# Two of the four heads' products of P by the inverse row sums move from GpSimd to VectorE

## The reference

```
scores = einsum(q, k) * 32 ** -0.5          # the first has 4 heads of k and v, each for 4 of q
scores = where(causal, scores, -inf)
attn   = softmax(scores, axis=-1)
out    = einsum(attn, v)                    # then @ Wo, added to x
```

## Time and profile before

| | |
|---|---|
| median of three runs | 3520.3 us (3517.94 to 3524.21) |
| profiled execution | 3521.41 us, of which the span of the core is 3519.6 us |
| stage a0 (22 to 457 us of the span) | 435 us, PE busy 353.4, DVE 172.3, ACT 258.8, POOL 315.8 |
| stage a1 (883 to 1360 us) | 477 us, PE busy 418.8, DVE 176.0, ACT 276.0, POOL 319.1 |

### The profile page before, as it was taken

One profiled execution on the slowest core, in us unless ns is written; L12 is line 12 of the kernel. 1 busy time (PEld: TensorE's weight loads), 2 busy tenths in 40 slices (PEclk: granted clock), 3 DMA queues, 4 the chain that ended last, 5 costly groups with the idle time before them and its releaser, 6 DMA issues. The chain is left out here.

```text
span 3519.6 us, 46857 instructions
## 1 busy us (share of the span) xinstructions
PE 3027.7 (86%) x16388; PEld 2286.1 (65%) x16388; DVE 1881.8 (53%) x5092; ACT 1556.4 (44%) x3598; POOL 1261.5 (36%) x1399
## 2 busy tenths in 40 slices
PE   6788789997899985887868875998779999989999
PEld 4666567886666663544646754776367777768887
DVE  4434267777443334323466667665577787753221
ACT  4666656665566554123322225443545555541000
POOL 4877823222576673000016761000033333313222
PEclk8889899998999996889989987999889999999999
DMA  2000030102000003021110011000300000020000
GB/s 84 1 1 1 1 119 31 32 31 78 1 1 1 1 1 123 26 72 59 66 57 4 4 42 57 1 1 34 113 1 1 1 1 1 1 99 12 12 13 13
DMA packets 65872, 105.51 MB, mean 30 GB/s; under 512 B 9315, under 2 KB 29795, under 8 KB 65509
## 3 DMA queue, kind: packets, MB, share of 16 engines
q1 hardware_dynamic: 65222, 102.41, 8.4%
q0 software_dynamic: 416, 0.10, 0.0%
HBM read 89.75 MB, written 12.85 MB: 29 GB/s over the span
## 5 line engine op out<-in xcount | busy, mean ns | idle before, releaser
L661 POOL TENSOR_SCALAR a_P<-a_P,a_rec 128x384 f32<-128x384 f32 (+3 forms) x512 | 548.2, 1093 | 241.4 <-DVE a_rec L816 241.4
L402 ACT ACTIVATE tree_value<-tree_bit,table_lut,tree_step 128x256 f32<-128x256 uint8 x496 | 275.7, 595 | 138.0 <-DVE tree_value L416 71.9
L416 DVE COPY_PREDICATED tree_value<-tree_bit,tree_value 128x256 f32<-128x256 uint8 x434 | 234.3, 547 | 133.7 <-ACT tree_value L402 105.3
L893 PE MATMUL bank<-ident,a_P 128*128 128x128 f32 x1280 | 200.4, 307 | 114.8 <-POOL a_P L661 112.5
L810 DVE CUSTOM_DVE_ANT_0 a_P<-bank,a_causal 128x384 f32<-128x384 f32 (+3 forms) x512 | 221.6, 480 | 123.3 <-PE bank L883 123.3
L732 ACT ACTIVATE a_P<-a_P,a_low 128x384 f32<-128x384 f32 (+3 forms) x512 | 281.2, 556 | 13.4 <-DVE a_low L810 13.3
L101 PE MATMUL bank<-f_xT_hi,f_w_hi 128*128 128x512 f32 (+1 forms) x704 | 276.1, 392 | 8.1 <-DVE f_w_lo L1145 8.1
L1069 POOL CAST f_h_hi<-f_sg 128x512 fp32r<-128x512 f32 (+1 forms) x88 | 85.1, 967 | 548.4 <-DVE f_sg L1166 277.6
L102 PE MATMUL bank<-f_xT_hi,f_w_lo 128*128 128x512 f32 (+1 forms) x704 | 275.7, 392 | 0.0
L103 PE MATMUL bank<-f_xT_lo,f_w_hi 128*128 128x512 f32 (+1 forms) x704 | 275.5, 391 | 0.0
L893 PEld LDWEIGHTS bank<-ident,a_P 128*128 128x128 f32 x1280 | 164.5, 158 | 149.1 <-POOL a_P L661 124.6
(11 more groups left out here) (451 smaller groups left out, 7824.3 us busy)
## 6 DMA issues: line engine op xcount, KB each, us to landing
f_w_raw<-in_f_w SPq DMA_DIRECT2D x11, 768.0 KB, 12.5
f_w_raw<-table_w SPq DMA_DIRECT2D x11, 768.0 KB, 11.2
tree_idx<-in_f_idx SPq DMA_DIRECT2D x62, 128.0 KB, 2.1
table_w<-tree_value SPq DMA_DIRECT2D x62, 128.0 KB, 1.7
x_res<-in_x SPq DMA_DIRECT2D x4, 1024.0 KB, 11.0
m_piece<-in_m_wq SPq DMA_DIRECT2D x2, 2048.0 KB, 12.2
m_piece<-in_m_wo SPq DMA_DIRECT2D x2, 2048.0 KB, 8.7
m_piece<-in_m_w_gate SPq DMA_DIRECT2D x2, 2048.0 KB, 10.8
```

The lines of the kernel that those rows point to most:

```text
L402: act.activation(prog.tree_value[(h + to) % 4][:, :], prog.tree_bit[h % 2][0][:, :], ACT.Identity, bias=prog.table_lut[:, 2 * k:2 * k + 1] ...
L416: dve.copy_predicated(prog.tree_value[(h + keep) % 4][:, :], prog.tree_bit[h % 2][bit][:, :], prog.tree_value[(h + other) % 4][:, :]).then ...
L661: last = pool.tensor_scalar(Pr[j][:, g, col:col + n], Pr[j][:, g, col:col + n], rec[:, j, i, g:g + 1], None, ALU.mult)
L893: last = pe.transpose(ps[J.bank(key)][:, g * P:(g + 1) * P], Pr[j][:, g, col + kt * P:col + (kt + 1) * P], prog.ident[:, :])
```

## The change

On POOL the loop over heads at L661 now runs over heads 2 and 3 only. On DVE the entry `rec`, behind the reciprocal, waits for it and multiplies P of heads 0 and 1, in place, with the same instruction that POOL used, and counts a new semaphore `p_scaled_dve`. The first transpose of a chunk waits for both. The entry for DVE's products stands inside `rec`, so `low` of n + 2 for heads 2 and 3 now comes after them.

```diff
@@ gpsimd
                     pool.wait_ge(*c_rec(0, at + 1))
-                    for g in range(G):
+                    for g in range(G // 2, G):
                         for i, (col, qt) in enumerate(PARTS[j]):
                             n = (qt + 1) * P
                             last = pool.tensor_scalar(Pr[j][:, g, col:col + n], Pr[j][:, g, col:col + n], rec[:, j, i, g:g + 1], None, ALU.mult)
@@ vector
                     dve.wait_ge(*c_exp(0, G * (at + 1)))
                     dve.reciprocal(rec[:, j, 0:parts, :], total[:, j, 0:parts, :]).then_inc(c_rec.sem, 1)
+                    dve.wait_ge(*c_rec(0, at + 1))
+                    for g in range(G // 2):
+                        for i, (col, qt) in enumerate(PARTS[j]):
+                            n = (qt + 1) * P
+                            last = dve.tensor_scalar(Pr[j][:, g, col:col + n], Pr[j][:, g, col:col + n], rec[:, j, i, g:g + 1], None, ALU.mult)
+                    last.then_inc(c_own.sem, 1)
@@ tensor
                     if at == FIRST[3 * m + j]:
+                        pe.wait_ge(*c_own(0, 3 * m + j + 1))
                         pe.wait_ge(*c_scaled(0, 3 * m + j + 1))
```

More of the change, by code:

```diff
@@ L593, in attention32 @@
     c_whi, c_wlo, c_xhi, c_xlo = (prog.count(n) for n in ("w_hi", "w_lo", "xT_hi", "xT_lo"))
-    c_qk, c_exp, c_scaled, c_pv = (prog.count(n) for n in ("qk_hi", "p_exp", "p_scaled", "pv"))
+    c_qk, c_exp, c_scaled, c_own, c_pv = (prog.count(n) for n in ("qk_hi", "p_exp", "p_scaled", "p_scaled_dve", "pv"))
     c_ot_hi, c_ot = (prog.count(n) for n in ("ot_hi", "ot_lo"))
@@ L942, in attention32 @@
     c_scaled.advance(CHUNKS)
+    c_own.advance(CHUNKS)
     c_pv.advance((PER - 1) * NU)
```

## The result

The changed kernel took 3396.6 us (median of four runs, 3395.84 to 3405.19), against 3521.9 us before: a ratio of 0.9651, 95% interval 0.9633 to 0.9669. That is 125 us less; the prediction was 3415 us, 106 less, with a range of 3375 to 3480.

What follows compares the result with a forecast made beforehand. PE was taken as the bound, idle in both attentions mostly for POOL's products of P. Waits 96 plus clock 25 less cost 15 gave 106 us saved, 3521.4 - 106 = 3415 us; range 3375 to 3480.

Steps and rivals of the forecast that it cites:

- What bounds it: In both attention stages, a0 and a1, PE's waits for POOL's product of P make 112.5 of 140 us idle.
- The price on DVE: DVE's new products beside POOL: 0.78 us each at 512 columns; 146 us over 32 units, 91 if nothing collides.
- The rule that spoke against it: Shared SBUF ports as exclusive lock: each DVE product in a0 and a1 would wait out a POOL product of 1.57 us.
- the rival of the port: DVE's product is held for a whole POOL product, nothing gained at j = 0; 3495 us, 3480 to 3513; chance 0.10.
- the slower one: Same port block, over 4.2 us at j = 0, delaying `low` and the banks; +26 us, 3546; chance 0.08.
- What ends the wait next: At a chunk j = 0, late `low` and score products end PE's wait, which shrinks from 4.22 to 1.6 us.
- The cost: Delayed `low` where PE has work but needs the bank: 15 us, bounds 0 and 51.
- the clock: PE's granted clock in a0 and a1 recovers as waits go: 25 us saved, a third of 78; bounds 0 and 60.
- the sign that the prediction gave: PE's granted clock rises above 0.90 in a0 and above 0.95 in a1.
- The upper bound: Whole kernel: largest forecast saving, given as 145 us (3375 us) and as 112 + 60 - 25.
- The moved wait: PE is fed late by ACT or DVE's in-order waits for ACT's Q and K; 3465 to 3480 us; chance 0.12.

Runs made afterwards that it cites:

- the removal alone: Changed kernel with DVE multiplying nothing, P of heads 0 and 1 left undivided, POOL keeping heads 2 and 3; 0.9568 of the kernel before, 3371 us.
- the added delay: Changed kernel plus two DVE instructions of 0.65 us per chunk between the products and `low` of heads 2 and 3; 0.9744 of the kernel before.

## Why the prediction was right, and where it was off

**What bounds it.** Right. PE waited for POOL's products, and taking two of four away takes 96 us of PE's idleness away, as the removal alone shows. That the removal's waits fit so exactly is partly luck; the mechanism is not, since with one head on DVE the waits at the transposes are 62 us again.

**The price on DVE.** A product of 512 columns beside POOL was put at 0.78 us; the pair took 1.32, so 0.66. POOL's pair was put at 3.3 us and took 3.40. DVE's busy time grew by 114 us where 146 were reckoned and 91 would have been the price without collisions. The nearest row (the normalising of the earlier trace rows) was the right kind of row; it overstated the pair by 0.24 us.

**The rule that spoke against it.** The Trainium skill (SBUF — State Buffer, section "SBUF: two separate sides") has DVE's two-port form blocked for a whole GpSimd instruction. Beside POOL's products the trace disagrees: DVE's second product takes 0.92 us and not 1.57 + 0.48. Whether DVE was in that form there, no row says. Beside a POOL instruction that reads two tiles the block does show, and the prediction did not foresee it for this form. In stage a1 of the changed kernel:

```profile
936.58 1.30 DVE L821 TENSOR_SCALAR a_P<-a_P,a_rec 128x384 f32<-128x384 f32 x1
...
935.13 2.54 POOL L672 TENSOR_TENSOR x_res<-x_res,a_bo 128x512 f32<-128x512 f32 x2
```

A product of 384 columns takes 0.41 us without a neighbour; this one took 1.30 us and ended 0.2 us after POOL's second addition (937.88 and 937.67). Only seven of the 256 products are held like that, so for this kernel the rival of the port is dead, with the slower one that needed it. The latter's mechanism, a late `low`, is real, as the added delay showed, but at j = 0 the products took 1.32 us, under a third of the 4.2 us from which it would decide.

**What ends the wait next.** Right, step by step: `low` for heads 2 and 3, then the score products, within 0.1 us of POOL. The cost was put at 15 us of waiting. In waits it was 13.2 (23.9 instead of 10.7), and in PE's idle time 13 (96 us gone with the removal alone, 83 with the change).

**The step that was mis-sized is the clock.** The prediction took 25 us, a third of the 78 that a clock that never falls would give. The change brought 39, and the removal alone 46. Those 14 us more, 3 us in other stages and 2 us of idleness (83 for 96 - 15) make 125 of 106. Most of it is in a0, where the busy time fell by 30 us; in a1 it fell by 9, and its clock is 0.95, no more than on the edge of the sign that the prediction gave.

**Two terms were off in opposite directions.** Taken by medians, the removal alone saved some 152 us, where 96 + 25 = 121 were reckoned, and the products cost some 30, where 15 were. That the sum came within 19 us is in part luck. By the profiled executions the cost is 22 us, of which 13 are idleness, and the prediction's cost had no term for the clock. The fall of the clock was treated as a bonus that is mostly given back. It is better read as part of the waits' price, but not as a fixed share: for each us less of idleness the busy time fell by 0.6 us in a0 and 0.3 in a1, and the added delay cost a0 7 us of idleness and 16 of busy time. The removal's 7 us over the change's 39 are hardly more than the clock does from run to run.

**The upper bound.** The prediction ends its range of savings with 112 + 60 - 25. That is 147 and not 145, and its 25 is neither the cost's estimate (15) nor one of its bounds (0 and 51); nothing shown supports it.

**The moved wait.** It didn't come. DVE's waits for ACT's Q shrank from 66.6 to 19.7 us in a0 and from 56.3 to 21.7 in a1, while those for ACT's K in a1 stayed (70.6 and 74.1). Its wait for the cast behind POOL's products fell in a0 from 47.6 to 24.5, by half, as POOL's products did.

**What stays open.** How the 30 us of the products divide between the delay of `low` and the collisions is not settled: the added delay costs 30 us for 1.3 us, but it was added on top of one that had used up the slack. Two heads behind `low` avoid the delay but not the collisions, and brought 0.2 to 0.3%, within the intervals; there the products themselves also come later. That three heads behind `low` are as fast as the removal alone says that most of both can be avoided together, though POOL has only one head there and two in the removal. No run avoids the collisions alone.

## What to carry to other kernels

- When an engine's work is moved off the path, look at what the receiving engine does right behind the place of insertion and who waits for that. Of the two places tried, the better one was 1.5 us later, behind the instructions that free PE's banks; with one head left on POOL, its share was also nearly over before the two could collide.
- A split between two engines has its own optimum for each place in the order: two and three heads were equal ahead of `low`, three clearly better behind it. Try the two together.
- When PE's granted clock is below 1.00 in a stage that waits, a shorter wait can also shorten the work around it: here 83 us less idleness came with 39 us less busy time. The share differs from stage to stage, so give it a wide range.

## What the runs showed of the hardware that was not expected

Adding 180 needless transposes inside PE's waits made stage a0 8.2 us shorter, with the granted clock up from 0.86 to 0.91. So work for nothing can bring more than it costs; the expectation ahead of that run had this, the prediction had not.

DVE's products of 512 columns took 0.49 us and 0.92 us as first and second beside POOL's, and 1.5 us beside POOL's two-input addition, against 0.42 to 0.48 us alone. What DVE's instruction costs depended on what POOL was doing.

All products on DVE (0.969) was no faster than two on POOL (0.965 and 0.966), and clearly slower than one on POOL behind `low` (0.956), although a product of 512 columns takes DVE 0.42 us and POOL 1.57. The Trainium skill (GPSIMD Engine Reference, section "4.1 Engine selection") gives elementwise work to VectorE, and calls GpSimd's one-input work roughly line-rate. Per instruction VectorE is the faster here too, but by more than three times; for the program the slower engine's idle time was worth using.
